# A graph network of four layers on Trainium2: a quarter of the edges of the middle layers taken from SBUF by one-hot products

## The reference

```
_loop = jnp.arange(3125, dtype=jnp.int32)
src = jnp.concatenate([_s, _d, _loop])
dst = jnp.concatenate([_d, _s, _loop])
_o = jnp.argsort(dst, stable=True)
...
x = _layernorm(x + _L0_gnn_ref(...))   # sum over edges of x[src] @ W[type 16], + x @ self_weight
x = _layernorm(x + _L1_gnn_ref(...))   # twice: h = tanh(sum of c[type 32] * h[src] @ basis_b (4 bases) + h @ loop_w + bias)
x = _layernorm(x + _L2_gnn_ref(...))   # relu((sum over edges of x[src]) @ W.T + b)
x = _layernorm(x + _L3_gnn_ref(...))   # attention over edges, 8 heads
```

## Time and profile before

| what | value |
|---|---|
| median of 3 runs | 2990.53 us (2988.95 to 3003.87) |
| span of the profiled execution | 2283.0 us |
| own time of the profiled execution | not given beside the span |
| instructions | 31899 |
| PE, DVE, POOL busy | 1623.0, 1513.0, 1629.8 us |
| chain that ended last | POOL 62%, issue 21%, PE 6%, DMA 6% |

### The profile page before, as it was taken

One profiled execution on the slowest core, in us unless ns is written; L12 is line 12 of the kernel. 1 busy time (PEld: TensorE's weight loads), 2 busy tenths in 40 slices (PEclk: granted clock), 3 DMA queues, 4 the chain that ended last, 5 costly groups with the idle time before them and its releaser, 6 DMA issues.

```text
span 2283.0 us, 31899 instructions
## 1 busy us (share of the span) xinstructions
PE 1623.0 (71%) x8447; PEld 1238.0 (54%) x8473; DVE 1513.0 (66%) x5097; ACT 433.1 (19%) x904; POOL 1629.8 (71%) x1690
## 2 busy tenths in 40 slices
PE   4777777775677676677465666766656989888886
PEld 3555555553555455555344444544435777777775
DVE  8776776775666666665355655555677878777775
ACT  0000000002000000000211111111255444444342
POOL 7777777775777777775677777777337777777771
PEclk9655555555555655655577777777885555555555
DMA  5233233231332333233423233333144434333331
GB/s 140 56 86 84 57 85 85 56 86 44 84 85 55 114 84 99 70 86 84 125 84 100 84 100 100 84 100 99 41 126 114 111 110 112 111 106 108 109 107 34
DMA packets 148261, 205.83 MB, mean 90 GB/s; under 512 B 47912, under 2 KB 110235, under 8 KB 147952
## 3 DMA queue, kind: packets, MB, share of 16 engines
q0 software_dynamic: 60032, 136.67, 22.1%
q1 hardware_dynamic: 86898, 65.12, 9.5%
q10 hardware_dynamic: 1154, 1.99, 0.3%
HBM read 170.89 MB, written 36.04 MB: 91 GB/s over the span
## 4 chain that ended last, share of the span: by engine, by line
POOL 62%; issue 21%; PE 6%; DMA 6%; DVE 3%; ACT 1%; DVEq 0%; POOLq 0%; another core or an unknown queue 0%; SPq 0%
POOL G L541 44%; POOL G L1426 18%; PE p_g L607 3%; DMA G<-in_x,idx 3%; DMA G<-h_d,idx 3%; PE p_d L653 1%; PE p_d L618 1%; PE p_o L638 0%; PE p_w L1493 0%; DVE XH L1208 0%; DVE work L1032 0%; DVE S L976 0%; DMA idx<-in_src 0%; DMA G<-kv_d,idx 0%; DVE work L1016 0%
## 5 line engine op out<-in xcount | busy, mean ns | idle before, releaser
L541 POOL DMA_INDIRECT G<-h_d,idx x832 | 792.0, 952 | 285.0 <-issue 261.3
L607 PE MATMUL p_g<-S,G 128*128 128x96 f32 (+1 forms) x2496 | 606.6, 389 | 465.4 <-DMA G<-h_d,idx 293.8
L607 PEld LDWEIGHTS p_g<-S,G 128*128 128x128 f32 x2496 | 526.1, 292 | 661.6 <-issue 302.5
L1426 POOL DMA_INDIRECT G<-kv_d,idx x416 | 421.3, 1013 | 159.9 <-issue 159.6
L541 POOL DMA_INDIRECT G<-in_x,idx x416 | 402.1, 967 | 132.3 <-issue 119.5
L1001 DVE TENSOR_SCALAR work<-iota_h,key_f 128x600 bf16<-128x600 f16 x416 | 168.0, 404 | 256.1 <-PE p_d L618 255.9
L976 DVE SCALAR_TENSOR_TENSOR S<-con,rel,shared 128x96 f32<-128x96 f32 (+1 forms) x1248 | 316.1, 293 | 0.7
L618 PE MATMUL p_d<-work 128*128 128x312 bf16 (+1 forms) x832 | 273.9, 431 | 22.2 <-DVE work L1016 21.1
L994 DVE TENSOR_TENSOR agg<-agg,p_g 128x96 f32 (+1 forms) x624 | 143.1, 229 | 146.4 <-PE p_g L607 121.3
L1092 DVE TENSOR_TENSOR work<-work,p_d 128x512 f32<-128x512 f32 (+1 forms) x168 | 104.5, 625 | 143.9 <-PE p_d L653 141.2
L1016 DVE TENSOR_TENSOR work<-work,p_d 128x312 f32 (+1 forms) x416 | 190.6, 458 | 13.1 <-issue 9.4
(11 more groups left out here) (250 smaller groups left out, 1969.6 us busy)
## 6 DMA issues: line engine op xcount, KB each, us to landing
work<-A_d SPq DMA_DIRECT2D x25, 800.0 KB, 4.6
A_d<-work SPq DMA_DIRECT2D x12, 1600.0 KB, 7.3
G<-h_d,idx POOLq DMA_INDIRECT x832, 2.5
G<-in_x,idx POOLq DMA_INDIRECT x416, 2.5
G<-kv_d,idx POOLq DMA_INDIRECT x416, 2.7
h_d<-XH SPq DMA_DIRECT2D x75, 64.0 KB
h_d<-in_x SPq DMA_DIRECT2D x2, 1600.0 KB, 7.7
QW<-q_d SPq DMA_DIRECT2D x104, 30.0 KB, 2.0
```

Source lines behind the costliest of these rows:

```text
L541: pool.indirect_dma_start(G[:, c % GRING, :], None, l.table, bass.IndirectOffsetOnAxis(ap=l.places[:, c:c + 1], axis=0)).then_inc(s_arr[g ...
L607: last = pe.matmul(p_g[:, g % PB, 0:width], G[:, c % GRING, :], S[:, c % (SRING * GR), 0:width], start=(k == 0), stop=(k == GR - 1))
L1426: pool.indirect_dma_start(G[:, c % KRING, :], None, d["kv"], bass.IndirectOffsetOnAxis(ap=idx[:, c:c + 1], axis=0)).then_inc(s_arr[c // QC ...
```

## The change

The 416 chunks are seen as NBLK = 13 periods of 32. In layers 1 and 2 the first 24 chunks of a period (12 groups) go as before; the last 8 chunks, 1024 edges, form a block that is not gathered. 13 x 12 = 156 groups, 312 chunks, remain.

- **Sorting, in layer 0.** The nodes are divided into BKT = 13 ranges of 256 (SPAN). For each block and range the edges whose source lies there form a bucket with 128 slots. `before_in_tile` and `ranks` number a block's edges within their bucket; `places_in` and `payload` put each edge's eight coefficients, its destination (relative to the block's base) and its source into its slot by products with one-hot matrices; the result stays in SBUF as `slots`, and the sources also go to DRAM as `low`.
- **Fetching.** A block's 13 buckets are worked in four parts of 4, 3, 3 and 3, one every three groups. SP loads the part's sources, spread over all partitions (`load_lows`); ACT makes one-hots of them as relu(1 - (source - node)^2) (`make_hots`, two squares and a relu); PE multiplies them with the layer's rows, which lie in SBUF, two tiles for a bucket (`fetch`), and ACT copies the result (`copy_picked`).
- **Summing.** DVE makes factors for the 128 slots of each bucket with a window of WB = 72 nodes and 4 bases, 288 columns (`block_factors`), PE sums the 13 buckets (`block_sums`), and DVE adds once per block (`block_add`).
- **The number of passes.** `flags` sets f_no, now also if a block spans over 71 nodes or if the count of any bucket, summed by `totals`, is above P = 128. Layers 1 and 2 then run more iterations, in which the blocks' slots are masked by f_ok and a second group of iterations (TWICE) takes a period's last chunks in place of the first. `iteration_start` is longer and runs in layer 1 too.
- The ring G falls from 40 to 26 chunks, the banks of p_g for the sums from 3 to 2, those of p_d for `dense` from 3 to 2. One-hots and counts of layer 1 go at the rate of 4 items in 3 groups. The padded edges get sources spread over the nodes in place of 0.

```diff
-GRING = 40
+GRING = 26
...
+NBLK = 13
+BC = 8
+PERIOD = EC // NBLK
+PGRP = PERIOD // GR
+PG = PGRP - BC // GR
+NGH = NBLK * PG
+WB = 72
+SPAN = 256
+BKT = math.ceil(NT * P / SPAN)
+PAY = 10
+PART = ((0, 4), (4, 7), (7, 10), (10, 13))
+NPART = NBLK * len(PART)
...
+        self.mixed = n > 0
+        self.ng = NGH if self.mixed else NG
...
+    def group(self, i):
+        return PGRP * (i // PG) + i % PG if self.mixed else i
...
-    def iterations(eng):
-        eng.wait_ge(s_fl, 9)
-        return eng.value_load(np_i[0:1, 1:2], min_val=1, max_val=400)
+    def iterations(eng, l):
+        eng.wait_ge(s_late, 1)
+        at = 3 if l.n == 1 else 1
+        return eng.value_load(np_i[0:1, at:at + 1], min_val=1, max_val=300 * l.n)
...
+                pool.wait_ge(s_it, IT_IDX)
+            for n in range(l.ng * GR):
+                i = n // GR
+                c = l.group(i) * GR + n % GR
+                if i + 4 > GP and n % (4 * GR) == 0:
+                    pool.wait_ge(s_mm, i - GP + 4)
...
+        def fetch(l, n):
+            i, lo, hi = part_of(n)
+            pe.wait_ge(s_hots, n + 1)
+            if n > 0:
+                pe.wait_ge(s_got, n)
+            for k in range(hi - lo):
+                tiles = range(2 * (lo + k), min(2 * (lo + k) + 2, NT))
+                for t in tiles:
+                    last = pe.matmul(p_x[:, k * P:(k + 1) * P], hots[:, t % 2, k, :], l.x_in[:, t, :],
+                                     start=(t == tiles[0]), stop=(t == tiles[-1]))
+            last.then_inc(s_get, 1)
+
+        def block_sums(l, n):
+            i, lo, hi = part_of(n)
+            pe.wait_ge(s_got, n + 1)
+            pe.wait_ge(s_Sb, n + 1)
+            if lo == 0 and i > 0:
+                pe.wait_ge(s_blk, i)
+            for k in range(hi - lo):
+                last = pe.matmul(p_s[:, 0:l.nb * WB], picked[:, n % 2, k * P:(k + 1) * P], Sb[:, k, 0:l.nb * WB],
+                                 start=(lo + k == 0), stop=(lo + k == BKT - 1))
+            last.then_inc(s_bs2, 1)
+
...
+        def make_hots(n):
+            _, lo, hi = part_of(n)
+            act.wait_ge(s_lowb[n % 2], 16 * (n // 2 + 1))
+            if n > 0:
+                act.wait_ge(s_get, n)
+            for u in range(2):
+                last = act.activation(hots[:, u, 0:hi - lo, :].rearrange("p k e -> p (k e)"),
+                                      low_b[:, n % 2, 0:(hi - lo) * P], ACT.Square,
+                                      bias=con[:, C_P1 + u:C_P1 + u + 1], scale=1.0)
+            last.then_inc(s_sq, 1)
+            act.wait_ge(s_sq, n + 1)
+            here = hots[:, :, 0:hi - lo, :].rearrange("p u k e -> p u (k e)")
+            act.activation(here, here, ACT.Relu, bias=con[:, C_ONE:C_ONE + 1], scale=-1.0).then_inc(s_hots, 1)
+
+        def copy_picked(n):
+            _, lo, hi = part_of(n)
+            act.wait_ge(s_get, n + 1)
+            if n >= 2:
+                act.wait_ge(s_bs2, n - 1)
+            act.activation(picked[:, n % 2, 0:(hi - lo) * P], p_x[:, 0:(hi - lo) * P], ACT.Copy).then_inc(s_got, 1)
+
...
+        def block_factors(l, n, lo, hi):
+            i, first, _ = part_of(n)
+            if lo == 0 and n > 0:
+                dve.wait_ge(s_bs2, n)
+            f = l.f0 - 2
+            for k in range(lo, hi):
+                row = slots[:, i, first + k, :]
+                last = dve.scalar_tensor_tensor(Sb[:, k, 0:l.nb * WB].rearrange("p (b w) -> p b w", w=WB),
+                                                bc(con[:, C_I + 1:C_I + 1 + WB], 1, l.nb), row[:, PAY - 2:PAY - 1],
+                                                bc(row[:, f:f + l.nb], 2, WB), ALU.is_equal, ALU.mult)
+            return last
+
+        def block_add(l, i, g):
+            off = dve.snap(base_regs[i % 2 * (PG + 1) + PG], min_val=0, max_val=AGW - WB)
+            dve.wait_ge(s_added, g + 1)
+            dve.wait_ge(s_bs2, len(PART) * (i + 1))
+            at = agg[:, 0:l.nb, bass.ds(off, WB)]
+            dve.tensor_tensor(at, at, p_s[:, 0:l.nb * WB].rearrange("p (b w) -> p b w", w=WB),
+                              ALU.add).then_inc(s_blk, 1)
+
...
+        def totals():
+            pe.wait_ge(s_rank, ROUNDS)
+            for c in range(BC):
+                last = pe.matmul(p_x[:, 0:NBLK * BKT], order_b[:, P:2 * P], member[:, :, c, :], start=(c == 0),
+                                 stop=(c == BC - 1))
+            last.then_inc(s_tot, 1)
...
+        dve.tensor_scalar(n_p4, npass_f, 1.0, 2.0, ALU.add, ALU.mult)
...
+            dve.tensor_reduce(npf[:, N_CNT:N_CNT + 1], p_x[:, 0:NBLK * BKT], AX_X, ALU.max).then_inc(s_flag, 1)
+            dve.wait_ge(s_flag, ROUNDS + 1)
+            dve.scalar_tensor_tensor(f_no, npf[:, N_CNT:N_CNT + 1], float(P), npf[:, N_NF:N_NF + 1], ALU.is_gt,
+                                     ALU.max).then_inc(s_flag, 1)
...
+            dve.scalar_tensor_tensor(MORE, n_p4, -1.0, f_no, ALU.add, ALU.mult)
+            dve.tensor_scalar(MOST, n_p4, 2.0, -1.0, ALU.mult, ALU.add).then_inc(s_flag, 1)
+            dve.wait_ge(s_flag, ROUNDS + 3)
+            dve.tensor_tensor(MOST, MOST, f_no, ALU.mult).then_inc(s_flag, 1)
+            dve.wait_ge(s_flag, ROUNDS + 4)
+            dve.tensor_scalar(np_i[:, 2:3], f_no[0:1], float(NT), None, ALU.mult)
+            dve.tensor_scalar(np_i[:, 3:4], MORE[0:1], 1.0, None, ALU.add)
+            dve.tensor_scalar(np_i[:, 1:2], MOST[0:1], 1.0, None, ALU.add).then_inc(s_late, 1)
+
...
+            dve.scalar_tensor_tensor(PAS, Z, n_m4, itc[:], ALU.mult, ALU.add).then_inc(s_it, 1)
+            dve.tensor_scalar(GOF, Z, float(NP), float(NP * (l.n - 1)), ALU.mult, ALU.add).then_inc(s_it, 1)
+            dve.wait_ge(s_it, 4)
+            dve.tensor_scalar(TWICE, PAS, n_p2, None, ALU.is_ge).then_inc(s_it, 1)
             dve.tensor_scalar(idx2[:], idx[:], GOF, None, ALU.add).then_inc(s_it, 1)
...
+            rest = spread_out(rel[:])[:, :, BC:PERIOD - BC]
+            dve.tensor_scalar(rest, rest, FAR, None, ALU.subtract)
...
+    src[E:] = np.arange(EP - E) * P % N
...
```

More of the change, by code:

```diff
@@ L97 @@
 SPLIT_LAG = (5, 6, 6, 7, 7)
-DENSE = sorted((READY[t] + 9 + j, t, j) for t in range(NT) for j in range(DBLK))
+DENSE = sorted((READY_H[t] + 9 + j, t, j) for t in range(NT) for j in range(DBLK))
 DENSE_AT = {}
@@ L485, in sums_body @@
                 sp.wait_ge(s_fill, 32)
+            else:
+                for k in range(2):
+                    sp.wait_ge(s_lowst[k], 16 * len(range(k, NBLK, 2)))
             for k in range(2):
@@ L655, in dense, with before_in_tile @@
             last.then_inc(s_dm, 1)
+        def before_in_tile(r):
+            nb = min(ROUND, NBLK - r * ROUND)
+            blocks = slice(r * ROUND, r * ROUND + nb)
+            if r == 0:
+                pe.wait_ge(s_memb, 4)
+            else:
+                pe.wait_ge(s_rank, r)
+            out = p_x[:, 0:nb * BC * BKT].rearrange("p (i c k) -> p i c k", i=nb, c=BC)
+            pe.matmul(p_x[:, 0:nb * BC * BKT], order_b[:, 0:P], member[:, blocks].rearrange("p i c k -> p (i c k)"),
+                      start=True, stop=False)
+            for k in range(BC - 1):
+                for i in range(nb):
+                    last = pe.matmul(out[:, i, k + 1:BC, :], order_b[:, P:2 * P],
+                                     bc(member[:, r * ROUND + i, k, :], 1, BC - 1 - k), start=False,
+                                     stop=(k == BC - 2 and i == nb - 1))
+            last.then_inc(s_pre, 1)
@@ new lines, in totals, with payload @@
+        def totals():
[4 more added lines that the diff above has]
+            last.then_inc(s_tot, 1)
+        def payload(i):
+            pe.wait_ge(s_good, i + 1)
+            if i > 0:
+                pe.wait_ge(s_low, i)
+            for c in range(BC):
+                last = pe.matmul(p_x[:, 0:BKT * PAY], place[:, c, :], goods[:, c].rearrange("p k f -> p (k f)"),
+                                 start=(c == 0), stop=(c == BC - 1))
+            last.then_inc(s_pay, 1)
@@ L658, in sums_body @@
             here = pe.snap(turn, min_val=0, max_val=1000)
-            landed = [here * (16 * GR * len(range(k, NG, GP))) for k in (0, GP - 1)]
+            if l.mixed:
+                landed = here * (16 * GR * (NGH // GP)) + npass * (16 * GR * ((NG - NGH) // GP))
+            else:
+                landed = here * (16 * GR * (NG // GP))
             if l.n == 2:
-                pe.wait_ge(s_it, 19)
+                pe.wait_ge(s_it, IT_ALL)
             coefs = turned = 0
```

542 lines of the change are left out of this document (392 added, 150 removed).

## The result

The changed kernel took 9462.74 us (median of 4 runs, 9435.48 to 9493.96), the kernel before, run beside it, 2989.74 us (4 runs, 2988.27 to 3003.87): 3.154 times as long, interval 3.1452 to 3.1627. Forecast were 7790 us and a range of 6950 to 9400. The sign and the twelve passes came as forecast. The time lies 63 us above the range, 1673 us above the forecast.

The account below looks back on a forecast made before the run. The prediction took POOL's gathers, one each 1.25 us, to bound the kernel before. Layer 0, four and eight passes of 490 us, 51 and attention's 591 made 7085; plus 707.5, 7790 us, range 6950 to 9400.

Parts of the forecast that it names:

- The number of passes: Layers 1 and 2: overfull buckets (fullest 153, ten of thirteen blocks above 128) set f_no to 1, giving 4 and 8 passes.
- I sum in spans, and add 707.5 unchanged: Whole kernel: the 707.5 us between span 2283.0 and median 2990.5 lie outside the span and are added unchanged.
- Rival (b): Whole kernel: what lies outside the span grows with it, 7085 x 1.31 = 9280 us; chance 0.17.
- The sum of spans: Whole kernel: 563 + 4 x 490 + 8 x 490 + 51 + 591 = 7085 us.
- Layer 0 563: Layer 0: its 548 us stay and the sorting adds 15 (bounds 0 and 76).
- 470 + 20: A pass of layer 1: about 470 us of work and waits plus 20 beyond its gathers, 490 (bounds 414 and 660).
- 450 + 40: A pass of layer 2: about 450 us with waits plus 40 for its end and start, 490 (bounds 430 and 775).
- The lockstep: Passes: every third group block_factors on DVE waits for the preceding block_sums on PE; 83 us a layer 1 pass, high clock.
- The clock: Passes of layers 1 and 2: PE is granted 0.9, so its work takes 378 us in layer 1 and 431 in layer 2.
- Rival (c): The passes: PE stays at 1.2 GHz, as in attention, giving 10750 us; chance 0.06.
- Rival (a): The twelve passes: gathers alone stay the bound, 414 us a pass in layer 1, 430 in layer 2, total 6990; chance 0.12.
- Rival (d): Layers 1 and 2: f_no stays 0, one pass each, span 2185, time 2890 us, faster by 3.3%; chance 0.06.

Follow-up runs that it names:

- e1: The changed kernel with the bucket test's bound raised from 128 to 1024, so one pass each, edges past slot 128 left out: 2240.06 us, 0.9794 of before.
- e2: The changed kernel with blocks of six chunks for eight, a block's parts at groups 0, 3, 6, 9, all edges kept: 2243.75 us, 0.9804 of before.
- e3: The changed kernel, unchanged, run on a chip at the faster level: 7382.65 us, 3.2296 times the kernel before.
- e4: e1 with the block work of layers 1 and 2 left out, so the blocks' edges are not summed: 2051.78 us, 0.8974 of the kernel before.
- e5: e2 with the window of a block's sums cut from 72 to 52 nodes, computing all: 2178.19 us, 0.9531 of the kernel before.
- e6: e5 with two sets of block factors, so DVE waits for the block sums of one part earlier: 2168.76 us, 0.9478 of the kernel before.
- e7: e6 with the second of the two products of each fetched bucket left out, output incomplete: 2147.24 us, 0.9396 of the kernel before.

## Why the prediction was right or wrong

**The number of passes** was right, by a count on the inputs and not by luck, and decided the case: 4 and 8, because ten of thirteen blocks overflow a bucket. e1 shows that this one test is worth 5143 of the 7383 us, and e2 that it goes away with blocks of six chunks.

**The step that failed** is "I sum in spans, and add 707.5 unchanged". There is nothing between span and time (1.9 us). The trace read was of an execution at 2285 us, the median given was of another level, and this level stretches the whole span: layer 0 from 561 to 699 us (1.25 times), passes of layer 1 from 530 to 629 (1.19), of layer 2 from 505 to 672 (1.33), attention from 587 to 842 (1.43). Rival (b) multiplied by 1.31 and gave 9280, 2% below the result, but by luck: its reason (a part outside that grows, a span near 7000) was not the true one, for the span is 9492; it should have been "the profile is of another level than the median", and it deserved more than 0.17. With both in hand, 2990.5 against 2283.0, scaling was the plainer reading: a fixed 707 us outside a span of 2283 had no row for it.

**The sum of spans** was 7085, and e3's span is 7373.9, 4% more. Layer 0 563 (561 measured) and attention 591 (587) were right. The 289 us that miss lie in the passes: layer 1 took 535.5, 529.3, 525.4 and 526.8 us, 157 above 4 x 490, and layer 2 504 to 513, in all 138 above 8 x 490. Inside a pass the terms were nearly right (487.5 and 444.7 for 470 and 450); what was mis-sized is the end of a pass, "470 + 20" and "450 + 40": POOL's idle there is 45 to 47 us in layer 1 and 63 to 68 in layer 2 in e3, 714 in the twelve passes, where the prediction had 400 with all else that lies beyond the gathers. e4 shows that the block work itself lengthens that end, from 19 to 45 us in layer 1.

**The lockstep** was the right wait with the wrong worth. The waits of the whole of e3:

```profile
POOL G L691 <- issue: 1173.5, 3849, 0.4
DVE Sb L1302 <- PE p_d L868: 791.7, 468, 7.3
POOL G L691 <- PE p_g L760: 774.3, 298, 8.6
POOL G L691 <- DVE now L1473: 665.3, 12, 67.6
```

(The 665.3 are the eleven ends between passes and the 14.3 us ahead of the first.) 791.7 us in 12 passes is 66 a pass, near the 83 forecast. In e5 it was 50 a pass, and removing it (e6) brought 5. That a pass came out near 470 all the same means that the 83 stood for something else. The gain of e5, a little more than either engine's own saving, the wait that moved in e6 and the quarter that came in e7 point to an alternation of PE and DVE inside a group, which the prediction had no term for; no run took work off DVE alone, so it is argued and not shown.

**The clock**: taken 0.9, measured 0.87 in layer 1 and 0.92 in layer 2 at the faster level. Rival (c), PE at 1.2 GHz, fell. Attention was granted 0.50 in every trace, with PE busy for 476 of 587 us, while the passes had 0.87 with PE busy for 415 of 535. By the Trainium skill (TensorE: Matmul & The Clock Gate, Part 1) activity releases the throttle; the passes agree with this, attention does not, so busy share alone does not tell which stretch gets 2.4 GHz.

**Rival (a)**, the gathers alone, fell: it needed 414 a pass. e4 reaches that only with the block work gone. **Rival (d)** fell by its own condition, and where e1 removes that condition its gain was half of what it was priced at (47 us for 98).

**What stays open** is what makes the slower level. It is not the speed of the transfers or of DVE, ACT and POOL: the packets of the gathers' queue took 12.3% of 9492 us at the slower level and 17.1% of 7374 at the faster, a gather keeps POOL for 976 ns and 972, and DVE's busy time is 5284 us and 5268. The two spans are 2118 us apart. PE's busy time is 635 us longer, at the lower granted clock, and how much of that lengthens the span no run shows. What else grows are waits that end with PE's matmuls, and some of these come singly where neither the trace nor the program has anything for them to wait for. That would fit instructions that reach PE late, but this was only argued.

The best version is e6: 2168.76 us, 5.2% less than the kernel before and 3.4 times as fast as the change as it stood.

## What to carry to other kernels

Where a kernel falls back to more passes when a bucket is full, count the fullest bucket on the inputs with their structure (here the self loops, whose sources lie as close together as their destinations) before pricing anything else: 153 edges in 128 slots cost 5 ms. Here a span and a time that differed by a quarter were of two executions at different levels; where no row shows anything outside the span, a forecast in spans is to be scaled, not topped up. And when an edit takes the bound off an engine, price the end of each pass anew, and ask of a wait what stands right behind it before giving it a worth.

## What the runs showed of the hardware

The same program takes 2285 or 2990 us, and 7380 or 9460. For the changed kernel both levels have a trace: the busy times of DVE, ACT and POOL are equal, PE's is 6485 us for 5849, and the stages stretch by 1.19 to 1.43. In attention the difference is a stall of some 10 us in each 30 us, at one place of the loop. And leaving out 312 of the 2405 matmul records of a pass, which took 34 us off their line, lowered PE's busy time by 12.7 us only, while the granted clock of the pass went from 0.90 to 0.86.
